# Self attention on one Trainium2 core: row-maximum pass a quarter stage further ahead, value and sum products in four batches a stage

## What is computed

```python
xn = layer_norm(x, ln0_w, ln0_b)
q, k, v = jnp.split(xn @ qkv_w.T, 3, axis=-1)      # 16 heads of 32
attn = jnp.einsum('bhnd,bhmd->bhnm', q, k) * HEAD_DIM ** (-0.5)
attn = jax.nn.softmax(attn, axis=-1)               # over all 2048 keys
sa = merge(jnp.einsum('bhnm,bhmd->bhnd', attn, v)) @ sa_proj_w.T
x = x + sa
```

## Time and profile before

| | |
|---|---|
| median of three runs | 4059.58 us (4033.05 to 4073.68) |
| profiled execution, span | 4101.8 us |
| all instructions, busy: TensorE | 91% |
| VectorE | 59% |
| ScalarE | 40% |
| GpSimd | 42% |

### The profile page before, as it was taken

The page is one execution under the profiler, slowest core; times in us unless marked ns, Lnnn a source line. Parts: engine busy times, 40 slices in busy tenths (PEclk is TensorE's granted clock), DMA queues, the critical chain, the costliest instruction groups (busy, mean ns, idle before and its releaser), DMA issues. The chain is left out here.

```text
span 4101.8 us, 58306 instructions
## 1 busy us (share of the span) xinstructions
PE 3723.8 (91%) x17160; PEld 2144.2 (52%) x17160; DVE 2422.7 (59%) x3586; ACT 1647.5 (40%) x2887; POOL 1734.4 (42%) x415
## 2 busy tenths in 40 slices
PE   7998999999999999999999859779898659999999
PEld 6884444444444444444444247534432548888887
DVE  4437787887888887878888434435544553222222
ACT  3222555565655555555555523223334232111111
POOL 0003776786777677777776712212333310000000
PEclk9997999999999999999999879855555779999999
DMA  4445131221303213131221044576661573111110
GB/s 169 179 159 124 38 85 35 68 62 47 90 24 83 53 50 80 32 87 42 63 65 30 9 158 170 176 152 129 131 143 39 206 268 111 65 41 41 41 41 21
DMA packets 197952, 370.22 MB, mean 90 GB/s; under 512 B 28707, under 2 KB 53049, under 8 KB 188653
## 3 DMA queue, kind: packets, MB, share of 16 engines
q1 hardware_dynamic: 197868, 369.15, 31.9%
HBM read 248.68 MB, written 119.34 MB: 90 GB/s over the span
## 5 line engine op out<-in xcount | busy, mean ns | idle before, releaser
L1118 DVE TENSOR_REDUCE self_part_max<-self_first 128x1 f32<-128x512 f32 x2048 | 1281.5, 684 | 360.4 <-PE self_first L963 359.8
L1072 ACT ACTIVATE self_expo<-self_second 128x512 f32<-128x512 f32 x2048 | 1106.9, 601 | 893.1 <-PE self_second L992 881.4
L937 POOL TENSOR_TENSOR self_pair_sum<-self_expo 128x2048 f32<-128x2048 f32 x256 | 1173.5, 4589 | 549.8 <-ACT self_expo L1072 549.8
L963 PE MATMUL self_first<-self_k_move,self_q_hold 96*128 96x512 f32 x2048 | 877.4, 456 | 80.3 <-DVE self_part_max L1118 67.6
L992 PE MATMUL self_second<-self_q_move,self_k_hold 98*128 (+1 forms) x2048 | 830.0, 418 | 23.5 <-DMA self_q_move<-self_max_low 14.2
L963 PEld LDWEIGHTS self_first<-self_k_move,self_q_hold 96*128 96x128 f32 x2048 | 393.6, 198 | 696.7 <-DVE self_part_max L1118 580.3
L1009 PE MATMUL self_weighted<-self_expo,self_v_sb 128*32 128x512 f32 x4096 | 550.3, 609 | 0.0
L992 PEld LDWEIGHTS self_second<-self_q_move,self_k_hold 98*128 98x128 f32 x2048 | 393.1, 195 | 214.0 <-ACT self_expo L1072 110.7
L1482 DVE CAST mlp_h_high<-mlp_h 128x512 fp32r<-128x512 f32 x128 | 54.9, 429 | 506.9 <-PE mlp_out_sum L61 506.9
L1457 ACT ACTIVATE mlp_h<-mlp_hidden_sum,mlp_b_col 128x512 f32<-128x512 f32 x128 | 88.1, 688 | 603.4 <-PE mlp_hidden_sum L61 603.4
L937 POOL TENSOR_TENSOR cross_pair_sum<-cross_expo 77x2048 f32<-77x2048 f32 x32 | 144.8, 4524 | 357.5 <-ACT cross_expo L1072 357.5
(11 more groups left out here) (165 smaller groups left out, 4351.1 us busy)
## 6 DMA issues: line engine op xcount, KB each, us to landing
self_q_hold<-q_t SPq DMA_DIRECT2D x384, 64.0 KB, 2.0
self_k_move<-k_t SPq DMA_DIRECT2D x96, 256.0 KB
self_q_move<-q_t SPq DMA_DIRECT2D x96, 256.0 KB, 4.3
self_k_hold<-k_t SPq DMA_DIRECT2D x96, 256.0 KB, 4.3
cross_q_hold<-cq_t SPq DMA_DIRECT2D x24, 1024.0 KB, 12.1
cross_q_move<-cq_t SPq DMA_DIRECT2D x24, 1024.0 KB, 14.6
qkv_x<-in_x SPq DMA_DIRECT2D x8, 1024.0 KB, 5.5
v<-qkv_v_sb SPq DMA_DIRECT2D x32, 256.0 KB, 2.0
```

The costliest lines, as they stand in the source:

```text
L937: nc.gpsimd.tensor_tensor(pair_sum[0:width, p % pair_slots], expo[0:width, t % p_slots], expo[0:width, (t + 1) % p_slots], ALU.add).then_i ...
L963: mm = nc.tensor.matmul(first[:, n % ring], q_hold[0:score_rows, a, s * P:(s + 1) * P], k_move[0:score_rows, a, k0:k0 + TOK], start=True, ...
L1072: nc.scalar.activation(expo[0:width, t % p_slots, a], second[0:width, n % ring], ACT.Exp, scale=scale).then_inc(exp_done, 1)
L1118: nc.vector.tensor_reduce(part_max[:, a * r_tiles * SUB + s, k:k + 1], first[:, n % ring], AX_X, ALU.max).then_inc(first_read, 1)
```

## The change

The self attention gets a function of its own, `self_phase`; the cross attention keeps `attention_phase`.

- A stage is four **blocks** of four key tiles. In a block first-pass and second-pass matmuls alternate, sixteen of each, all through the stage. Behind them comes a **batch**: the `weigh` groups of the four key tiles of the block before, and one or two `add_up` groups (`sums_after`): six groups in blocks 0 and 2, five in 1 and 3.
- The first pass runs 80 matmuls ahead instead of 64: blocks 0 to 2 do the last 48 of stage i + 1, block 3 the first 16 of stage i + 2. So the maxima of stage i + 1 are complete at the end of block 2, and the transpose and the split come in block 3 behind the second reduction. The transpose has a place of its own in the three banks (`turn_slot`).
- `take_total` and the SBUF tile `sums` are gone. VectorE inverts in four pieces of 128 columns, reading and writing the PSUM bank `total`, and multiplies `total` (PSUM) with `unscaled` (SBUF). Pieces and multiplication stand in block 1 of the next stage, each between two reductions.
- `total` is used six times a stage in four batches; GpSimd's ten operations stay in kind and number, and a pair's slot is free when its sum has been read.
- The loads follow the same rules, in the order of the new waits.

The added function cut to what orders the work (a line of dots where lines are left out):

```diff
--- before.py
+++ after.py
+def self_phase(nc, name, q_t, k_t, v, out, batches):
+    tokens, features = q_t.shape[2], q_t.shape[1]
+    keys = tokens // batches
+    heads = HEADS_PER_GROUP
+    groups_per_batch = features // P
+    stages_per_group = keys // TOK
+    groups = batches * groups_per_batch
+    stages = groups * stages_per_group
+    scale = 1.0 / math.sqrt(HEAD_DIM)
+    base = 3 * HEAD_DIM
+    exp_rows = base + 2
+    n_k = keys // P
+    n_items = heads * SUB * (keys // TOK)
+    per_head = n_items // heads
+    n_max = heads * SUB
+    n_reads = n_items + 1
+    n_seconds = heads * n_k
+    blocks = n_k // 4
+    per_block = 4 * heads
+    firsts_per_block = n_items // blocks
+    ahead = per_head
+    turn_after = 2
+    ring = 3
+    p_slots = 8
+    pair_slots = 4
+    pieces = 4
+    k_set = n_k // 4
...
+    pool_ops = [("pair", 0), ("pair", 1), ("pair", 2), ("merge", 1), ("pair", 3), ("pair", 4), ("pair", 5), ("merge", 4),
+                ("pair", 6), ("pair", 7)]
+    summed = [0, 1, 3, 4, 6, 7]
+    sum_ready = [pool_ops.index(("merge", p) if ("merge", p) in pool_ops else ("pair", p)) + 1 for p in summed]
+    n_sums = len(summed)
+    sums_after = {0: [(-1, 4), (-1, 5)], 1: [(0, 0)], 2: [(0, 1), (0, 2)], 3: [(0, 3)]}
+    slot_sum = {0: [0, 3], 1: [1], 2: [4], 3: [2, 5]}
+
+    items = [(a, s, k0) for a in range(heads) for s in range(SUB) for k0 in range(0, keys, TOK)]
+    in_ring = [0, 1] + [(n + turn_after) % ring for n in range(turn_after, n_items)]
+    turn_slot = turn_after % ring
...
+    first_of = [[] for _ in range(blocks)]
+    for n in range(n_items):
+        at = n + ahead
+        first_of[n // firsts_per_block].append((1, at) if at < n_items else (2, at - n_items))
...
+        first = m.psum("first", [P, ring, TOK])
+        second = m.psum("second", [P, ring, TOK])
+        weighted = m.psum("weighted", [P, TOK])
+        total = m.psum("total", [P, TOK])
...
+                def load_max(i):
+                    ge(sp, first_read, reads_until_turned(i), alone=True)
+                    for row, src in ((base, max_high), (base + 1, max_low)):
+                        sp.dma_start(q_move[row:row + 1, i % 2].rearrange("o a (s t) -> o (a s) t", t=P).bitcast(F32),
+                                     src[:].bitcast(F32)).then_inc(max_loaded, 16)
...
+                    if has_next:
+                        ge(sp, second_done, n_seconds * i, alone=True)
+                        ge(sp, q_move_loaded, 48 * (i + 1), alone=True)
+                        load_q_move(i + 1)
+                    heads_free(0)
+                    if qt == 0 and number != 0:
+                        ge(sp, weighted_done, n_k * i, alone=True)
+                        load_v(g, 3)
+                    k_free(0)
+                    heads_free(1)
+                    v_free(0)
+                    if number != 0:
+                        store_out(i - 1)
+                    k_free(1)
+                    heads_free(2)
+                    v_free(1)
+                    k_free(2)
+                    heads_free(3)
+                    if has_next:
+                        load_max(i + 1)
+                    v_free(2)
+                    k_free(3)
...
+                def add_pairs(i):
+                    for at, (what, p) in enumerate(pool_ops):
+                        if what == "pair":
+                            t = 2 * p
+                            ge(pool, exp_done, n_seconds * i + heads * (t + 2))
+                            before = [n for n in slot_sum[p % pair_slots] if summed[n] < p]
+                            if before:
+                                ge(pool, total_done, n_sums * i + before[-1] + 1)
+                            else:
+                                ge(pool, total_done, n_sums * (i - 1) + slot_sum[p % pair_slots][-1] + 1)
+                            nc.gpsimd.tensor_tensor(pair_sum[:, p % pair_slots], expo[:, t % p_slots],
+                                                    expo[:, (t + 1) % p_slots], ALU.add).then_inc(pool_done, 1)
+                        else:
+                            ge(pool, pool_done, len(pool_ops) * i + at)
+                            nc.gpsimd.tensor_tensor(pair_sum[:, p % pair_slots], pair_sum[:, p % pair_slots],
+                                                    pair_sum[:, (p + 1) % pair_slots], ALU.add).then_inc(pool_done, 1)
...
+                def first_pass(i, n):
+                    a, s, k0 = items[n]
+                    if n % per_head == 0:
+                        ge(pe, q_hold_loaded[a], 48 * (i + 1))
+                        ge(pe, k_move_loaded[a], 48 * (i // stages_per_group + 1))
+                    ge(pe, first_read, slot_free(i, in_ring[n], n))
+                    nc.tensor.matmul(first[:, in_ring[n]], q_hold[0:base, a, s * P:(s + 1) * P],
+                                     k_move[0:base, a, k0:k0 + TOK], start=True, stop=True).then_inc(first_done, 1)
...
+                def turn_max(i):
+                    ge(pe, first_read, slot_free(i + 1, turn_slot, turn_after))
+                    ge(pe, row_max_done, i + 1)
+                    nc.tensor.transpose(first[0:n_max, turn_slot, 0:P], row_max[:], identity[:]).then_inc(turned, 1)
...
+                def batch(i, j, with_last, with_this):
+                    for t in range(4 * j - 4, 4 * j):
+                        if t >= 0 and with_this:
+                            weigh(i, t)
+                        if t < 0 and with_last:
+                            weigh(i - 1, t + n_k)
+                    for of, n in sums_after.get(j, ()):
+                        if with_this if of == 0 else with_last:
+                            add_up(i + of, n)
+
+                def period(i, with_last, with_next, with_after):
+                    for j in range(blocks):
+                        for at in range(per_block):
+                            of, n = first_of[j][at]
+                            if with_next if of == 1 else with_after:
+                                first_pass(i + of, n)
+                            if of == 2 and n == turn_after - 1 and with_next:
+                                turn_max(i + 1)
+                            second_pass(i, j * per_block + at)
+                        batch(i, j, with_last, True)
+
+                pe.wait_ge(ident_done, 2)
+                pe.wait_ge(ones_done, 1)
+                for n in range(n_items):
+                    first_pass(0, n)
+                for n in range(turn_after):
+                    first_pass(1, n)
+                turn_max(0)
+                for n in range(turn_after, ahead):
+                    first_pass(1, n)
+                pe.wait_ge(rows_set, 3)
+                period(0, False, True, True)
+                with pe.Fori(1, stages - 2) as i:
+                    period(i, True, True, True)
+                period(stages - 2, True, True, False)
+                period(stages - 1, True, False, False)
+                batch(stages, 0, True, False)
...
+                def take_weighted(i):
+                    ge(act, weighted_done, n_k * (i + 1))
+                    ge(act, mean_done, i)
+                    nc.scalar.activation(unscaled[:], weighted[:], ACT.Copy).then_inc(weighted_read, 1)
+
+                def period(i, with_last):
+                    for n in range(n_seconds):
+                        exponential(i, n)
+                        if n == per_block + 1 and with_last:
+                            take_weighted(i - 1)
...
+                    if n == n_items - 1:
+                        ge(dve, first_read, reads_until(i, n))
+                        ge(dve, turned, i)
+                        nc.vector.tensor_reduce(row_max[:], part_max[:], AX_X, ALU.max).then_inc(row_max_done, 1)
+
+                def split_max(i):
+                    ge(dve, max_loaded, 32 * i)
+                    ge(dve, turned, i + 1)
+                    nc.vector.tensor_copy(max_high[:], first[0:n_max, turn_slot, 0:P]).then_inc(max_high_done, 1)
+                    ge(dve, max_high_done, i + 1)
+                    nc.vector.tensor_tensor(max_low[:], first[0:n_max, turn_slot, 0:P], max_high[:].bitcast(F32),
+                                            ALU.subtract).then_inc(first_read, 1)
+
+                def invert(i, part):
+                    if part == 0:
+                        ge(dve, total_done, n_sums * (i + 1))
+                    cols = slice(part * (TOK // pieces), (part + 1) * (TOK // pieces))
+                    nc.vector.reciprocal(total[:, cols], total[:, cols]).then_inc(inverse_done, 1)
+
+                def divide(i):
+                    ge(dve, inverse_done, pieces * (i + 1))
+                    ge(dve, weighted_read, i + 1)
+                    ge(dve, out_stored, 16 * i)
+                    nc.vector.tensor_tensor(mean[:], total[:], unscaled[:], ALU.mult).then_inc(mean_done, 1)
+
+                def period(i, with_last, with_next, with_after):
```

(22 more changed lines are left out.)

226 lines of the change are left out of this document (added).

## The result

The change made the kernel slower: 4120.77 us (median of 4 runs, 4117.44 to 4122.3) against 4058.32 us (4 runs, 4033.05 to 4073.68), a ratio of 1.0169 with a 95% interval of 1.0129 to 1.0209. I had forecast 4019 us, a range up to 4105, and gave "slower" a chance of 0.18. Every ratio in this document comes from the fast runs alone, without those over 1.5% above the fastest of their kernel, and so differs a little from the quotient of the medians beside it.

What follows compares the result with a forecast made beforehand. VectorE's 0.60 us pitch was taken to pace the blocks: 56.3 us of blocks and batches, 4.0 of inverse and multiplication, 0.7 of transpose made a 61.0 us stage. In all 41 us less than 4059.58: 4019 us, range 3975 to 4105.

Steps and rivals of the forecast that it cites:

- The sum of the blocks: Four blocks of sixteen pairs paced by VectorE, each with its batch of five or six groups: 56.3 us a stage.
- transpose and split: In block 3 behind the second reduction, delaying the third reduction from 1.74 to 2.43 us: 0.7 us a stage.
- pieces: Four inverse pieces on VectorE in block 1, 0.85 us each, 3.4 us a stage.
- The multiplication: On VectorE in block 1, with one operand in PSUM: 0.62 us, where line 1154 had a median of 7.68.
- The sum of the stage: Blocks and batches 56.3, inverse and multiplication 4.0, transpose and split 0.7: 61.0 us.
- rival C: TensorE's clock falls in block 1 among the inverses: about 2.5 us a stage, 4056 or 4091 us; chance 0.13.
- the base: The forecast gain of 41 us was taken from the runs' median 4059.58 us, giving 4019; from the profile's 4101.8, 4061.
- rival F: Timed runs of before seldom have the multiplication collide with GpSimd's sums, so the gain is gone: 4060 us; chance 0.14.
- the collision: Line 1154's multiplication reads two SBUF tensors while GpSimd's sums run: median 7.68 us, against 0.69 free of them.
- D: Inverse in PSUM is dear: 1.71 us a piece, block 1 grows by 3.4 us, 4121 us; chance 0.11.

Runs made afterwards that it cites:

- a_spread: Kernel after with the inverse pieces behind every fourth reduction of block 1 instead of every second, multiplication behind the 16th: 4013.61 us, ratio 0.9983 to before.
- a_refill: Kernel after with the first ten second-pass matmuls of block 1 issued twice: 4081.21 us, ratio 1.017 to before.
- a_best: a_half2 with the transpose and split of the maxima moved from block 3 into the batch ending block 2: 3918.89 us, ratio 0.9706 to before.
- a_half2: a_half with two inverse pieces behind block 0, one mid block 1, one with the multiplication at its end: 3932.34 us, ratio 0.9738 to before.
- a_half: Kernel after with batch 0's sums first, inverse behind block 0, multiplication behind block 1, each batch cut in two: 3934.39 us, ratio 0.9772 to before.

## Why the prediction was wrong

**The sum of the blocks was right.** Sixteen pairs to the batch 9.12 (forecast 9.15), batches 5.29 and 4.43 (5.35 and 4.48), transpose and split 0.69 (0.7), pieces 0.80 each (0.85), multiplication 0.60 (0.62). With the clock held, these make 57.2 + 3.2 = 60.4 us a stage, where I had 61.0. GpSimd was not late.

**The multiplication was right.** One operand in PSUM took it from a median of 7.68 us to 0.68. By the rule of the Trainium skill (SBUF — State Buffer, Who interferes with whom) that I weighed, the trace agrees.

**The step that failed is the clock of block 1.** The sum of the stage has no term for it: it takes every pair at the full clock. The fall stood only in rival C, which I believed too little (0.13). Its price was "about 2.5 us if it lasts to the batch"; measured 2.1 to 2.2 us a stage. That the total was near is in part luck: I had put 2.2 us into the block and the small rest into the batch; it was 1.0 in the block and 1.2 in the batch. (C's 4091 for all stages should have been 4019 + 30 x 2.5 = 4094.) The reason for the low chance was that the engine had been idle for 3.48 us before a fall, and that no gap here would be longer than about 1 us. No gap was, 0.68 at the longest, and the clock fell in all the stages that have the pieces and a row-maximum pass. I had one example of a fall and took its length for a condition. The trace of before had no stretch in which the pairs came two at a time with stops between (TensorE's stops in its steady stages are 0.1 us, or single ones of 1.2 to 3.5), so it could not say that such a stretch is safe. The Trainium skill (TensorE: Matmul & The Clock Gate, A second HAM failure mode: psum-queue depth-cycling) describes this pattern, short stops between groups of matmuls; here the trace agrees, and I should have let it move the chance.

In the profiled executions: the last multiplication ended at 2353.7 us before and at 2369.7 after, 16 us later instead of 41 us earlier, 57 us of miss. 29 stages at 62.58 - 61.0 make 46 of them (2.1 of clock less the 0.6 that I had counted too much). The other 11 are what remains outside the steady stages; the clock fell there too, from 2295 us on.

**The second step that failed is the base.** I took 41 us from the median 4059.58 of before, though I named rival F, that timed runs collide less, at 0.14. The times bear it out, and the granted clocks of the timed runs with them: the gap between profile and timed runs goes with the collision and leaves with it. The expected gain was measured on an execution with most of its multiplications at 7.7 us, and the timed ones had less to give back. So both misses add up: 4061 became 4115.7 in the profile, 55 us; and the timed runs of after lie 5 above that, where I had set them 42 below. 55 + 5 + 42 = 102, the 4120.77 - 4019. With the clock alone mended, 30 x 2.1 = 63 us less, the kernel after would be at about 4058, which is the time of before: F's figure. a_spread shows that nearly directly, with a stage of 59.03 us and yet no difference to before.

**D was wrong, though its time is nearly exact.** It gave 4121 us from pieces of 1.71 us; they add 0.80. Whoever looks only at the total would take the inverse to be dear.

What stays open: how the timed executions of before get past the collision that the profiled ones meet, what sets the first of a series apart, and how the fall of the clock depends on the pattern of stops. a_spread, with one stop for four pairs, and a_refill, with ten matmuls more, say only that less stopping was enough here. That a_best could go on falling to 54.8 us without the wait for the multiplication was only argued.

## What to carry to other kernels

Work put onto the engine that paces a matmul stretch costs its own time and, if it makes TensorE stop over and over, the clock on top: here 3.2 us of inverses cost 5.4. Put it where that engine waits anyway; the same pieces behind the sums of a batch cost nothing and turned 1.7% slower into 1.7% faster. And before a gain is taken from a median, see that the profiled execution is like the timed ones: where a duration has two values by a matter of phase, profile and median can stand for two different kernels.

## What the runs showed of the hardware

- TensorE's granted clock fell to 0.50, the 1.2 GHz level, in stages 1 to 30 of the kernel after, behind stops of 0.68 us at most; the engine had been doing two pairs of 512-column matmuls every 2.00 us. With four pairs between stops of the same length (a_spread) it stayed at 1.00.
- Ten more matmuls a stage made the kernel about 40 us faster (4081.21 against 4120.77, measured apart; 4078.8 against 4115.7 in the profiles).
- Groups of four column-tiled products cost 0.87 us one behind another, the figure by which batches of five and six came within 0.06 us of their forecast.
- A reciprocal of 128x128 in PSUM adds 0.80 us to a run of reductions (901 to 966 ns each), half the 1.71 of 256 columns in SBUF.
- Three profiled executions of the kernel before took 4083 to 4102 us at a granted clock of 0.891 to 0.893, where the timed medians were 4032 to 4058 and single timed runs reached 3992.89 us at 0.902. The kernels without the collision lay nearer to their profiles: within 2.4 us for six of them, 4.5 to 7.8 for a_half2, the kernel after and a_half.
